# Attention to the last feed-forward of a two-layer block: first weights split early, rows normalised and two slices run per 256 rows

## Chip, cores and metric

One core of one Trainium2 chip. The metric is the device time of one execution in microseconds, median of the runs shown; less is better.

## The reference

512 rows (2 batches of 256) of width 512 go through two layers. Only the last two steps bear on the change:

```
x = x + L1_attention(layernorm(x), ctx)   # 32 query heads, 8 key and value heads of 128, 512 context rows a batch
x = x + L1_ffn(layernorm(x))              # out = (silu(x @ gate.T * s) * (x @ up.T * s)) @ down.T * s, 1376 inner columns
```

Layer 0 ahead of them is an attention with 8-bit rounding and a feed-forward with block-scaled rounding; the change leaves both alone.

## The kernel before, in words

The order of work is written out by hand, one program for each engine, joined by semaphores: TensorE (`pe`), ScalarE (`act`), VectorE (`dve`), GpSimd (`pool`), and SyncE (`sp`), which issues all transfers into one queue. Each engine takes its instructions strictly in order.

**Precision.** Layer 1 keeps about full precision by splitting each operand in two: a high part, rounded to fp32r, and a low part, raw minus high. `three` (L633 to L637) makes three matmuls of one product: high by high, high by low, low by high. Its lines L635 to L637 are those of all such products; the operand names tell them apart. The weights are split by GpSimd: a `tensor_scalar` rounds the high part, a `tensor_tensor` subtracts.

**Attention.** 32 units, one per two heads and batch (`unit(U, u, g)`), run through a software pipeline of four steps j a unit; even units are batch 0, odd ones batch 1. In one step GpSimd scales the probabilities of one 128-row tile by 1 / row sum (L1083) and may split a weight (L1072 and L1074: `wq` and `wo`). TensorE turns the tile (L668), multiplies it with the values (`pT,vt`), and projects with `wo` (`wo_sb,oT`) three units later; each pair of units waits for its `wo` split (`wo_split`). VectorE adds the projection to the rows `X` (L1393), two 128-row tiles a unit. The last iterations (units 28 to 31 and three units of drain, up to index 34) stand unrolled behind a loop.

**From attention to feed-forward.** At unit 33 VectorE takes the statistics of tiles 0 and 1 (batch 0: unit 30 was the last to add to them), at unit 34 that of tile 2, then of tile 3. `standardise(0, 4)` works out 1 / deviation of all four tiles by a chain of 11 tiny operations (L1180 to L1185) and writes the normalised rows `xhat` (L1187). `turn_rows(3, ...)` turns them tile by tile in 16 transposes (L629) into banks 4 to 7, `rows_high` (ScalarE, L926) and `rows_low` (VectorE, L1377) write the two parts into `xt_again`.

**Last feed-forward.** The inner width goes in 11 slices of 128. `gate_up1(c, p)` makes gate and up of slice c for all 512 rows: 24 matmuls of 512 columns, weights stationary, into banks p and 2 + p. ScalarE applies silu (L1005), VectorE multiplies (L1470, which waits for `u1_sums`), ScalarE rounds (L1010), VectorE subtracts (L1472), and `down1(c, p)` adds slice c into banks 4 to 7 (12 matmuls). The order on TensorE is gate_up 0, gate_up 1, down 0, then gate_up 2, down 1, and so on. GpSimd splits slice c + 1's weights: `split_gate_up` (L1126, L1128) starts slice 2 when slice 0's up sums are done (`u1_sums`), `split_down` (L1133, L1135) waits for an earlier slice's down sums. `fw` holds two slices of split weights. It lies over buffers of the attention, so its first two splits wait for the end of the attention: slice 0 for the last values product (`pv_sums`), slice 1 for the normalised rows (`ln_ready`). SyncE loads the raw weights (`ffn_raw`, six transfers of 256 KB for slices 0 and 1, L447) behind all of the attention's.

## Time and profile before

| | us |
|---|---|
| median of 3 runs | 710.75 |
| lowest, highest | 708.11, 712.8 |
| profiled execution, its own time | 712.11 |
| its span, first to last instruction | 710.0 |
| TensorE busy | 672.4 (95%) |
| VectorE busy | 525.8 (74%) |
| GpSimd busy | 457.6 (64%) |
| mean granted TensorE clock | 0.990 |

In rows of the trace, PE is the matmul side of TensorE and PEld its weight loads, DVE is VectorE, ACT ScalarE, POOL GpSimd. Times are us from the span's start. The end of a matmul is modelled, so the distance between starts tells the pace, not the duration.

### The profile page before, as it was taken

How to read it: one execution, taken by the hardware profiler on the slowest of the kernel's cores; microseconds unless marked ns; L12 is line 12 of the kernel's file. 1: busy time of each engine (PE TensorE's matmuls, PEld its weight loads, DVE VectorE, ACT ScalarE, POOL GpSimd, SP SyncE). 2: the span in 40 equal slices, each digit the busy share in tenths (PEclk: the TensorE clock that was granted, in tenths of full speed). 3: DMA queues.
4: the chain of work that ended last, by engine and by line, in shares of the span. 5: the costliest groups of instructions: out<-in, count | busy, mean ns of one | idle time of the engine just before them, and what ended most of it. 6: DMA issues, size and time to landing. Idle time of an engine off the chain costs nothing.

```text
span 710.0 us, 10983 instructions
## 1 busy us (share of the span) xinstructions
PE 672.4 (95%) x3099; PEld 494.8 (70%) x3104; DVE 525.8 (74%) x1039; ACT 362.8 (51%) x684; POOL 457.6 (64%) x401
## 2 busy tenths in 40 slices
PE   4989899899989999999999999999999999699998
PEld 2434344444566788888888888888888887588886
DVE  4977799778678888888889888888888885631113
ACT  2659444542466666665665665565665663211111
POOL 2365716424269879778878779689688554556661
PEclk9989999999999999999999999999999999999999
DMA  9885322140232113023132141221221021122221
GB/s 338 274 309 184 127 90 75 45 163 18 98 109 80 68 61 118 31 66 112 30 101 77 37 126 44 83 80 44 88 74 40 21 65 55 54 81 89 89 89 60
DMA packets 39402, 67.25 MB, mean 95 GB/s; under 512 B 3664, under 2 KB 11984, under 8 KB 38352
## 3 DMA queue, kind: packets, MB, share of 16 engines
q1 hardware_dynamic: 39376, 66.93, 28.8%
q8 instruction: 13, 0.21, 0.1%
q14 instruction: 13, 0.11, 0.0%
HBM read 57.48 MB, written 9.44 MB: 94 GB/s over the span
## 4 chain that ended last, share of the span: by engine, by line
PE 77%; DVE 10%; issue 4%; POOL 4%; ACT 3%; DMA 1%; SPq 0%; POOLq 0%; ACTq 0%; DVEq 0%
PE ps L635 16%; PE ps L637 16%; PE ps L636 16%; PE ps L703 11%; PE ps L668 7%; PE ps L503 4%; PE ps L519 4%; PE ps L566 2%; DMA X<-in_x 1%; DVE mx_amax L1244 1%; DVE mx_raw L1262 1%; DVE f L1292 1%; DVE f_amax L1287 1%; POOL wq_sb L1074 1%; PE ps L497 1%
## 5 line engine op out<-in xcount | busy, mean ns | idle before, releaser
L1083 POOL TENSOR_SCALAR prob<-prob,rinv 128x512 f32<-128x512 f32 x128 | 89.4, 699 | 79.3 <-DVE rinv L1420 79.3
L944 ACT ACTIVATE prob<-ps,nmax 128x512 f32<-128x512 f32 x128 | 88.3, 690 | 97.4 <-DVE nmax L1413 94.9
L703 PE MATMUL ps<-xt,wq_sb 128*128 128x512 f32 x384 | 103.2, 393 | 3.8 <-DVE q_cos L1428 2.1
L955 ACT CAST pT<-ps 128x512 fp32r<-128x512 f32 x128 | 75.1, 587 | 52.0 <-PE ps L668 51.0
L1413 DVE CUSTOM_DVE_ANT_0 ps<-ps,mask_sb 128x512 f32<-128x512 f32 x128 | 87.9, 686 | 6.7 <-PE ps L637 6.3
L1434 DVE TENSOR_TENSOR pT<-ps,pT 128x512 fp32r<-128x512 f32 x128 | 86.3, 674 | 2.6 <-ACT pT L955 1.7
L703 PEld LDWEIGHTS ps<-xt,wq_sb 128*128 128x128 f32 x384 | 71.6, 188 | 21.9 <-issue 4.6
L668 PE MATMUL ps<-idf,prob 128*128 128x128 f32 x512 | 76.7, 272 | 0.3 <-POOL prob L1083 0.3
L668 PEld LDWEIGHTS ps<-idf,prob 128*128 128x128 f32 x512 | 63.8, 141 | 17.0 <-POOL prob L1083 1.0
L503 PE MATMUL ps<-ctxT,wk_sb 128*128 128x512 f32 x128 | 63.4, 636 | 7.7 <-DMA ctxT<-in_ctx_cols 6.7
L1035 POOL TENSOR_TENSOR mx_raw<-mx_raw,mx_r 128x2048 f32<-128x2048 f32 (+1 forms) x9 | 30.2, 3354 | 61.4 <-DVE mx_r L1252 61.4
L519 PE MATMUL ps<-wv_sb,ctxT 128*128 128x512 f32 x128 | 58.8, 610 | 5.3 <-DVE col L1228 2.8
L635 PE MATMUL ps<-pT,vt 128*128 128x512 f32 x128 | 61.1, 477 | 0.5 <-DVE pT L1434 0.5
L1086 POOL TENSOR_TENSOR q_swp<-q_swp,ropeQ 128x512 f32<-128x512 f32 x32 | 47.1, 1472 | 17.6 <-ACT q_swp L965 17.6
L1470 DVE SCALAR_TENSOR_TENSOR int<-ps,sc,silu 128x512 f32<-128x512 f32 x11 | 8.2, 750 | 59.6 <-PE ps L637 59.6
L635 PE MATMUL ps<-wo_sb,oT 128*128 128x512 f32 x128 | 50.2, 393 | 1.7 <-DVE oT L1401 1.4
L635 PE MATMUL ps<-kt,qt 128*128 128x512 f32 x128 | 50.6, 395 | 0.9 <-DVE kt L1447 0.5
L637 PE MATMUL ps<-pT,vt 128*128 128x512 f32 x128 | 50.8, 397 | 0.0
L636 PE MATMUL ps<-pT,vt 128*128 128x512 f32 x128 | 50.3, 393 | 0.0
L637 PE MATMUL ps<-kt,qt 128*128 128x512 f32 x128 | 50.2, 392 | 0.0
L1074 POOL TENSOR_TENSOR wo_sb<-wo_raw,wo_sb 128x512 fp32r<-128x512 f32 x32 | 48.4, 1511 | 2.7
L636 PE MATMUL ps<-wo_sb,oT 128*128 128x512 f32 x128 | 50.0, 391 | 0.0
(152 smaller groups left out, 1572.2 us busy)
## 6 DMA issues: line engine op xcount, KB each, us to landing
mx_raw<-in_mxw SPq DMA_DIRECT2D x8, 1024.0 KB, 6.7
wq_raw<-in_wq SPq DMA_DIRECT2D x32, 256.0 KB, 3.1
wo_raw<-in_wo SPq DMA_DIRECT2D x32, 256.0 KB, 2.7
k_scr<-k_st SPq DMA_DIRECT2D x16, 256.0 KB, 2.0
v_scr<-v_st SPq DMA_DIRECT2D x16, 256.0 KB, 2.3
kr<-k_scr SPq DMA_DIRECT2D x16, 256.0 KB, 2.9
vr<-v_scr SPq DMA_DIRECT2D x16, 256.0 KB, 3.7
kr_swp<-k_scr SPq DMA_DIRECT2D x28, 128.0 KB, 3.3
```

Source lines behind the costliest of these rows:

```text
L503: last = mm(bank(n), wk_sb[:, i % 2, k], ctxT[:, k, b * CTX:(b + 1) * CTX], start=(k == 0), stop=(k == KD - 1))
L519: last = mm(bank(n), ctxT[:, k, i * P:(i + 1) * P], wv_sb[:, k, h * 512:(h + 1) * 512], start=(k == 0), stop=(k == KD - 1))
L635: mm(out_ap, left[0], right[0], start=first, stop=False)
L636: mm(out_ap, left[0], right[1], start=False, stop=False)
L637: return mm(out_ap, left[1], right[0], start=False, stop=final)
L668: last = nc.tensor.transpose(bank(2 + i % 2)[:, k * P:(k + 1) * P], prob[:, i, k * P:(k + 1) * P], idf[:])
L703: last = mm(query_bank(H), wq_sb[:, par, l, k], xt[:, r, k], start=(n == 0), stop=(n == 11))
L944: nc.scalar.activation(prob[:, j], bank(j % 2), ACT.Exp, bias=nmax[:, j:j + 1], scale=-1.0, accum_out=rsum[:, j:j + 1]).then_inc(exps, 1)
L955: copy(pT[:, v % 2, 0, :, i * P:(i + 1) * P], bank(2 + i % 2).rearrange("p (k c) -> p k c", k=4)).then_inc(ph_ready, 1)
L1083: nc.gpsimd.tensor_scalar(prob[:, i], prob[:, i], rinv[:, i:i + 1], 1.0, ALU.mult, ALU.mult).then_inc(probs, 1)
L1413: nc.vector.tensor_tensor_reduce(out=bank(j % 2), in0=bank(j % 2), in1=mask_sb[:, 2 * (u % 2) + j % 2], scale=-1.0, scalar=BIG, op0=ALU.ad ...
L1434: tt(pT[:, v % 2, 1, :, i * P:(i + 1) * P], bank(2 + i % 2).rearrange("p (k c) -> p k c", k=4), pT[:, v % 2, 0, :, i * P:(i + 1) * P].bitc ...
```

## The change

It does four things.

- **Buffers.** `fw` is two tensors, `fw_even` (slices 0, 2, ...) over the raw and split query weights, and `fw_odd` over the raw keys and values. These are dead before the attention ends. `silu1`, `int1` and `int1s` lie between.
- **Transfers and splits.** SyncE issues the six loads of slices 0 and 1 ahead of the last four `wo` loads. GpSimd splits them one matrix at a time (`split_early`) in units 30 (steps 1, 3), 31 (1, 3) and 32 (1, 2), each behind that step's scaling, or behind the `wo` split.
- **Rows by batch.** VectorE normalises tiles 0 and 1 right after their statistics, ahead of the last two adds, and tiles 2 and 3 after the low parts of batch 0. Transposes (`turn_batch`), high and low parts go by batch, two 128-column groups of both tiles in one bank.
- **Slices 0 and 1 by batch.** `gate_up1_batch` makes gate and up of both slices for 256 rows of batch 0 (48 matmuls of 256 columns), then for batch 1; the sums of a slice are signalled at batch 1. From slice 2 on all is as before.

```diff
@@ SyncE
+            for c in range(2):
+                for m, w in enumerate((gate_w, up_w, down_w)):
+                    sp.dma_start(ffn_raw[:, c, m], w[c]).then_inc(fw_in[c], 16)
             for U in range(NUNIT - 4, NUNIT):
                 unit(U, U % 4, NKV - 1)
...
-            sp.wait_ge(ffn0_done, NT)
-            for c in range(2):
-                for m, w in enumerate((gate_w, up_w, down_w)):
-                    sp.dma_start(ffn_raw[:, c, m], w[c]).then_inc(fw_in[c], 16)
@@ TensorE
-            pe.wait_ge(proj_added, 2 * NUNIT)
-            turn_rows(3, ROW_BANKS[1])
+            def turn_batch(b):
+
+                pe.wait_ge(ln_ready, 3 * NT + 2 * b + 2)
+                for k in range(KD):
+                    for t in range(2):
+                        lo = (k % 2) * SEQ + t * P
+                        last = nc.tensor.transpose(bank(HALF_BANK[b] + k // 2)[:, lo:lo + P],
+                                                   xhat[:, 2 * b + t, k * P:(k + 1) * P], idf[:])
+                    if k % 2 == 1:
+                        last.then_inc(xh_turned, 1)
+
+            def gate_up1_batch(c, b):
+
+                pe.wait_ge(fw_split, 2 * c + 1)
+                cols = slice(b * SEQ, (b + 1) * SEQ)
+                for m, done in ((0, g1_sums), (1, u1_sums)):
+                    for k in range(KD):
+                        if c == 0 and m == 0:
+                            pe.wait_ge(xtl_ready, KD + 2 * b + k // 2 + 1)
+                        last = three(bank(2 * m + c)[:, cols], [fw[c][:, m, s, k * P:(k + 1) * P] for s in range(2)],
+                                     [xt_again[:, s, k, cols] for s in range(2)], k == 0, k == KD - 1)
+                    if b == 1:
+                        last.then_inc(done, 1)
...
-            gate_up1(0, 0)
-            gate_up1(1, 1)
+            for b in range(BATCH):
+                turn_batch(b)
+                gate_up1_batch(0, b)
+                gate_up1_batch(1, b)
             down1(0, 0)
@@ ScalarE
-            rows_high(1, xt_again)
+            for b in range(BATCH):
+                for n in range(2):
+                    act.wait_ge(xh_turned, KD + 2 * b + n + 1)
+                    copy(xt_again[:, 0, 2 * n:2 * n + 2, b * SEQ:(b + 1) * SEQ],
+                         bank(HALF_BANK[b] + n).rearrange("p (k c) -> p k c", k=2)).then_inc(xth_ready, 1)
@@ GpSimd
+            def split_early(U, j):
+
+                c, m = divmod({(30, 1): 0, (30, 3): 1, (31, 1): 2, (31, 3): 3, (32, 1): 4, (32, 2): 5}[U, j], 3)
+                if m == 0:
+                    pool.wait_ge(fw_in[c], 48)
+                if c == 0 and m == 0:
+                    pool.wait_ge(q_sums, NH)
+                if c == 1 and m == 0:
+                    pool.wait_ge(k_split, 2 * NKV)
+                    pool.wait_ge(v_split, 2 * NKV)
+                pool.sem_inc(pool_past_wait, 1)
+                nc.gpsimd.tensor_scalar(fw[c][:, m, 0], ffn_raw[:, c, m], 1.0, 1.0, ALU.mult, ALU.mult).then_inc(fwh_ready, 1)
+                pool.wait_ge(fwh_ready, 3 * c + m + 1)
+                low = tt(fw[c][:, m, 1], ffn_raw[:, c, m], fw[c][:, m, 0].bitcast(F32), ALU.subtract)
+                if m > 0:
+                    low.then_inc(fw_split, 1)
...
-            pool.wait_ge(pv_sums, NUNIT)
-            split_gate_up(0, 0, 0)
-            split_down(0, 0)
-            pool.wait_ge(ln_ready, 4 * NT)
-            split_gate_up(1, 1, 0)
-            split_down(1, 1)
@@ VectorE
+            def rows_low_again(b):
+                cols = slice(b * SEQ, (b + 1) * SEQ)
+                for n in range(2):
+                    dve.wait_ge(xth_ready, KD + 2 * b + n + 1)
+                    tt(xt_again[:, 1, 2 * n:2 * n + 2, cols], bank(HALF_BANK[b] + n).rearrange("p (k c) -> p k c", k=2),
+                       xt_again[:, 0, 2 * n:2 * n + 2, cols].bitcast(F32), ALU.subtract).then_inc(xtl_ready, 1)
...
                             row_stats(0)
                             row_stats(1)
                             aggregate(0, 2)
+                            standardise(0, 2)
...
             row_stats(NT - 1)
             aggregate(NT - 1, NT)
-            standardise(0, NT)
-            rows_low(1, xt_again)
+            rows_low_again(0)
+            standardise(2, NT)
+            rows_low_again(1)
```

What moves, engine by engine, at the places that matter. GpSimd in the unrolled units 29 to 32 and behind them, before; L1083 scales a tile's probabilities, L1072 and L1074 split one `wo`:

```order
L1072 TENSOR_SCALAR wo_sb<-wo_raw 128x512 [waits wo_in1]
L1074 TENSOR_TENSOR wo_sb<-wo_raw,wo_sb 128x512 [waits woh_ready]
L1083 TENSOR_SCALAR prob<-prob,rinv 128x512 [waits inverse] x4
L1072 TENSOR_SCALAR wo_sb<-wo_raw 128x512 [waits wo_in0,proj_sums]
L1074 TENSOR_TENSOR wo_sb<-wo_raw,wo_sb 128x512 [waits woh_ready]
L1083 TENSOR_SCALAR prob<-prob,rinv 128x512 [waits inverse] x2
L1072 TENSOR_SCALAR wo_sb<-wo_raw 128x512 [waits wo_in1]
L1074 TENSOR_TENSOR wo_sb<-wo_raw,wo_sb 128x512 [waits woh_ready]
L1126 TENSOR_SCALAR fw<-ffn_raw 128x512 [waits pv_sums,fw_in0]
```

And now, from the same `wo` split of unit 30's pair on (L1110 scales, L1099 and L1101 split `wo`):

```order
L1099 TENSOR_SCALAR wo_sb<-wo_raw 128x512 [waits wo_in1]
L1101 TENSOR_TENSOR wo_sb<-wo_raw,wo_sb 128x512 [waits woh_ready]
L1110 TENSOR_SCALAR prob<-prob,rinv 128x512 [waits inverse]
L1150 TENSOR_SCALAR fw_even<-ffn_raw 128x512
L1152 TENSOR_TENSOR fw_even<-ffn_raw,fw_even 128x512 [waits fwh_ready]
L1110 TENSOR_SCALAR prob<-prob,rinv 128x512 [waits inverse] x2
L1150 TENSOR_SCALAR fw_even<-ffn_raw 128x512
L1152 TENSOR_TENSOR fw_even<-ffn_raw,fw_even 128x512 [waits fwh_ready]
L1110 TENSOR_SCALAR prob<-prob,rinv 128x512 [waits inverse]
L1099 TENSOR_SCALAR wo_sb<-wo_raw 128x512 [waits wo_in0,proj_sums]
L1101 TENSOR_TENSOR wo_sb<-wo_raw,wo_sb 128x512 [waits woh_ready]
```

A cast and a subtraction of `fw_even` or `fw_odd` now stand between scalings, where before the first split of `fw` came behind all of them and waited for `pv_sums`.

VectorE behind the last low part of the attention's output (`oT`), before:

```order
L1171 BN_AGGR meanvar<-stats 128x2
L1393 TENSOR_TENSOR X<-ps,X 128x512 [waits proj_sums]
L1165 BN_STATS stats<-X 128x6 [waits proj_added]
L1171 BN_AGGR meanvar<-stats 128x2 [waits ln_step]
L1393 TENSOR_TENSOR X<-ps,X 128x512 [waits proj_sums]
L1165 BN_STATS stats<-X 128x6 [waits proj_added]
L1171 BN_AGGR meanvar<-stats 128x2 [waits ln_step]
L1180 TENSOR_SCALAR var_eps<-meanvar 128x4 [waits ln_step]
```

And now, from the end of the chain of tiny operations for tiles 0 and 1:

```order
L1225 SCALAR_TENSOR_TENSOR rstd<-newton,rstd 128x2 [waits ln_step]
L1227 TENSOR_SCALAR xhat<-X,meanvar,rstd 128x512 [waits ln_step]
L1227 TENSOR_SCALAR xhat<-X,meanvar,rstd 128x512
L1439 TENSOR_TENSOR X<-ps,X 128x512 [waits proj_sums]
L1205 BN_STATS stats<-X 128x6 [waits proj_added]
L1211 BN_AGGR meanvar<-stats 128x2 [waits ln_step]
L1439 TENSOR_TENSOR X<-ps,X 128x512 [waits proj_sums]
L1205 BN_STATS stats<-X 128x6 [waits proj_added]
L1211 BN_AGGR meanvar<-stats 128x2 [waits ln_step]
L1423 TENSOR_TENSOR xt_again<-ps,xt_again 128x2x256 [waits xth_ready] x2
L1220 TENSOR_SCALAR var_eps<-meanvar 128x2 [waits ln_step]
```

The normalised rows of tiles 0 and 1 come ahead of the two adds (L1439), and the second chain begins behind the low parts of batch 0.

TensorE behind its last projection matmul, before:

```order
L637 MATMUL ps<-wo_sb,oT 128x512
L629 MATMUL ps<-idf,xhat 128x128 [waits ln_ready,proj_added]
L629 MATMUL ps<-idf,xhat 128x128 x3
L629 MATMUL ps<-idf,xhat 128x128 [waits ln_ready]
L629 MATMUL ps<-idf,xhat 128x128 x3
```

And now (L756 turns the rows of batch 0):

```order
L639 MATMUL ps<-wo_sb,oT 128x512
L756 MATMUL ps<-idf,xhat 128x128 [waits ln_ready]
L756 MATMUL ps<-idf,xhat 128x128 x7
L637 MATMUL ps<-xt_again,fw_even 128x256 [waits xtl_ready,fw_split]
L638 MATMUL ps<-xt_again,fw_even 128x256
L639 MATMUL ps<-xt_again,fw_even 128x256
```

The first feed-forward matmul now waits for half of the rows (eight transposes instead of sixteen) and has 256 columns instead of 512.

## Rows read from the trace of the kernel before

**Rows 1.** The page, chain that ended last, by engine.

```profile
PE 77%; DVE 10%; issue 4%; POOL 4%; ACT 3%; DMA 1%; SPq 0%; POOLq 0%; ACTq 0%; DVEq 0%
```

**Rows 2.** TensorE's timeline: start us, us, instruction, count, idle before.

```profile
607.04 0.39 PE L637 MATMUL ps<-wo_sb,oT 128*128 128x512 f32 x1
612.16 3.31 PE L629 MATMUL ps<-idf,xhat 128*128 128x128 f32 x16 [4.74 <-DVE xhat L1187]
616.64 0.47 PE L635 MATMUL ps<-xt_again,fw 128*128 128x512 f32 x1 [1.17 <-DVE xt_again L1377]
...
627.64 0.39 PE L635 MATMUL ps<-fw,int1s 128*128 128x512 f32 x1
```

**Rows 3.** Weight loads (PEld) at the first feed-forward matmuls, timeline.

```profile
616.61 0.19 PEld L635 LDWEIGHTS ps<-xt_again,fw 128*128 128x128 f32 x1 [1.37 <-issue]
616.72 0.19 PEld L636 LDWEIGHTS ps<-xt_again,fw 128*128 128x128 f32 x1
```

**Rows 4.** Windows: busy (count) of PE, PEld, DVE, ACT, POOL; granted clock; DMA share, GB/s.

```profile
76.00:79.00 3.00, 0.30 (x2) 0.00 (x0) 3.00 (x3) 0.66 (x1) 2.69 (x1) 1.00 0.70 229
79.00:82.00 3.00, 2.88 (x4) 1.34 (x5) 2.93 (x6) 0.00 (x0) 0.00 (x0) 0.52 0.43 180
130.00:132.00 2.00, 0.00 (x0) 0.00 (x0) 1.58 (x1) 2.00 (x3) 1.77 (x2) 1.00 0.73 262
611.00:612.00 1.00, 0.00 (x0) 0.00 (x0) 0.90 (x5) 0.00 (x0) 0.00 (x0) 0.79 0.15 55
612.00:614.00 2.00, 1.84 (x9) 1.87 (x10) 1.39 (x4) 0.00 (x0) 0.39 (x1) 0.50 0.00 0
615.00:617.00 2.00, 0.83 (x6) 0.58 (x5) 1.20 (x2) 1.81 (x4) 2.00 (x1) 1.00 0.00 0
```

**Rows 5.** Timeline of VectorE, and ScalarE's copy, after the last projection.

```profile
605.58 0.25 DVE L1171 BATCH_NORM_AGGREGATE meanvar<-stats 128x2 f32<-128x6 f32 x2
606.10 0.69 DVE L1393 TENSOR_TENSOR X<-ps,X 128x512 f32<-128x512 f32 x1 [0.27 <-PE ps L637]
...
609.29 0.17 DVE L1180 TENSOR_SCALAR var_eps<-meanvar 128x4 f32<-128x4 f32 x1
...
611.47 1.92 DVE L1187 TENSOR_SCALAR xhat<-X,meanvar,rstd 128x512 f32<-128x512 f32 x4
...
615.18 2.05 ACT L926 CAST xt_again<-ps 128x512 fp32r<-128x512 f32 x4 [12.89 <-PE ps L629]
...
615.80 2.48 DVE L1377 TENSOR_TENSOR xt_again<-ps,xt_again 128x512 fp32r<-128x512 f32 x4 [2.42 <-ACT xt_again L926]
```

**Rows 6.** GpSimd's timeline in units 30 and 31, and wo's subtraction by the page.

```profile
577.71 0.69 POOL L1083 TENSOR_SCALAR prob<-prob,rinv 128x512 f32<-128x512 f32 x1 [2.43 <-DVE rinv L1420]
578.98 0.69 POOL L1083 TENSOR_SCALAR prob<-prob,rinv 128x512 f32<-128x512 f32 x1 [0.58 <-DVE rinv L1420]
579.65 0.62 POOL L1072 TENSOR_SCALAR wo_sb<-wo_raw 128x512 fp32r<-128x512 f32 x1
...
581.67 0.69 POOL L1083 TENSOR_SCALAR prob<-prob,rinv 128x512 f32<-128x512 f32 x1
...
L1074 POOL TENSOR_TENSOR wo_sb<-wo_raw,wo_sb 128x512 fp32r<-128x512 f32 x32 | 48.4, 1511 | 2.7
```

**Rows 7.** TensorE's timeline, last turned probabilities and first projection of unit 30.

```profile
594.61 0.60 PE L668 MATMUL ps<-idf,prob 128*128 128x128 f32 x4
...
598.65 0.50 PE L635 MATMUL ps<-wo_sb,oT 128*128 128x512 f32 x1
```

**Rows 8.** Slice 0: timeline of VectorE and GpSimd, and line L1472 (min/median/max ns).

```profile
622.49 0.75 DVE L1470 SCALAR_TENSOR_TENSOR int<-ps,sc,silu 128x512 f32<-128x512 f32 x1 [4.20 <-PE ps L637]
623.92 2.88 DVE L1472 TENSOR_TENSOR int1s<-int,int1s 128x512 fp32r<-128x512 f32 x1 [0.69 <-ACT int1s L1010]
...
623.86 2.40 POOL L1128 TENSOR_TENSOR fw<-ffn_raw,fw 128x1024 fp32r<-128x1024 f32 x1
...
L1472 DVE TENSOR_TENSOR int1s<-int,int1s x11: 691/693/2876, 623.9 to 702.8; 128x512 fp32r<-128x512 f32 x11
```

More of the change, by code:

```diff
@@ L35 @@
 CH = MXT * D
-ROW_BANKS = ([4, 5, 0, 7], [4, 5, 6, 7])
+ROW_BANKS = [4, 5, 0, 7]
+HALF_BANK = (0, 4)
 STEPS = (
@@ L207, in build @@
             int1s = sb("int1s", [P, 2, 2, 512], F32R, a)
+            fw_even = sb("fw_even", [P, 3, 2, D], F32R, a)
+            fw = (fw_even, fw_odd)
             res = sb("res", [P, NT, D], F32, a)
@@ L620, in _, with turn_rows @@
             late_keys(2, range(2, 4))
-            def turn_rows(turn, banks):
+            def turn_rows():
                 for t in range(NT):
-                    if turn == 2 and t == NT - 1:
+                    if t == NT - 1:
                         late_keys(3, range(KD))
-                    pe.wait_ge(ln_ready, 4 * turn + t + 1)
+                    pe.wait_ge(ln_ready, 2 * NT + t + 1)
                     for k in range(KD):
-                        last = nc.tensor.transpose(bank(banks[k])[:, t * P:(t + 1) * P], xhat[:, t, k * P:(k + 1) * P], idf[:])
+                        last = nc.tensor.transpose(bank(ROW_BANKS[k])[:, t * P:(t + 1) * P], xhat[:, t, k * P:(k + 1) * P], idf[:])
                         if t == NT - 1:
@@ L755, in gate_up1 @@
                     for k in range(KD):
-                        if isinstance(c, int) and c == 0 and m == 0:
-                            pe.wait_ge(xtl_ready, KD + k + 1)
-                        last = three(bank(2 * m + p), [fw[:, p, m, s, k * P:(k + 1) * P] for s in range(2)],
+                        last = three(bank(2 * m + p), [fw[p][:, m, s, k * P:(k + 1) * P] for s in range(2)],
                                      [xt_again[:, s, k] for s in range(2)], k == 0, k == KD - 1)
@@ L766, in down1 @@
                     last = three(bank(4 + t), [int1s[:, p, s, t * P:(t + 1) * P] for s in range(2)],
-                                 [fw[:, p, 2, s] for s in range(2)], isinstance(c, int) and c == 0, isinstance(c, int) and c == NI - 1)
+                                 [fw[p][:, 2, s] for s in range(2)], isinstance(c, int) and c == 0, isinstance(c, int) and c == NI - 1)
                     last.then_inc(d1_sums, 1)
-            gate_up1(0, 0)
-            gate_up1(1, 1)
+            for b in range(BATCH):
+                turn_batch(b)
+                gate_up1_batch(0, b)
+                gate_up1_batch(1, b)
             down1(0, 0)
@@ L921, in _, with rows_high @@
             copy_keys(*LATE_KEYS[2])
-            def rows_high(turn, dst):
+            def rows_high():
                 for k in range(KD):
-                    act.wait_ge(xh_turned, 4 * turn + k + 1)
-                    copy(dst[:, 0, k], bank(ROW_BANKS[turn][k])).then_inc(xth_ready, 1)
+                    act.wait_ge(xh_turned, k + 1)
+                    copy(xt[:, 0, k], bank(ROW_BANKS[k])).then_inc(xth_ready, 1)
             act.wait_ge(kr_in[0], 16)
@@ L1107, in unit @@
                         split(wo_sb[:, par // 2, par % 2, 0], wo_sb[:, par // 2, par % 2, 1], wo_raw[:, par % 2], woh_ready, wo_split, H + 1)
+                    if isinstance(U, int) and (U, j) in ((30, 1), (30, 3), (31, 1), (31, 3), (32, 1), (32, 2)):
+                        split_early(U, j)
+            def split_early(U, j):
[13 more added lines that the diff above has]
+                    low.then_inc(fw_split, 1)
             pool.wait_ge(wq_in[0], 16)
```

22 lines of the change are left out of this document (11 added, 11 removed).

## The prediction

> **What bounds the kernel now.** I read the page first: the chain that ended last runs through TensorE for 77% of the span [rows 1], so a change pays only where TensorE stands still or is slow. Then TensorE's timeline from the last attention work to the last feed-forward: it starts its last projection matmul at 607.04, gets its first transpose of the normalised rows at 612.16, needs 3.31 us for 16 of them, and starts the first feed-forward matmul after another 1.17 us idle [rows 2]. The weight-load row says when a matmul really begins: the second load starts with the first matmul, at 616.72 [rows 3]. The first down projection starts at 627.64 [rows 2]: 48 matmuls of 512 columns in 10.92 us, 0.2275 each. After that TensorE has no gap to the end, so the change is worth exactly what it moves this 627.64. Third, the granted clock [rows 4]: it fell near 611.6, stood at 0.50 (1.2 GHz) from 612 to 614, and was full from 615 on. Fourth, VectorE, which fills the 4.7 us hole: adds and statistics, a chain of tiny operations from 609.29 to 611.47, then four normalisations in 1.92 us [rows 5].
>
> **The change, part by part.**
>
> Early splits on GpSimd. Six splits of 128x512 move from behind the attention into units 30 to 32, and each delays the row scalings behind it. A scaling takes 0.67 (578.98 to 579.65), a split 2.02 (579.65 to 581.67) [rows 6]. From 577.71, GpSimd now has eight scalings (units 30 and 31) and six splits (E0 to E3 of the change, two of wo): 8 x 0.67 + 6 x 2.02 = 17.5, so the last scaling ends at 595.2. TensorE transposed it at 594.61 [rows 7]: 0.6 late, 0.7 with the signal. Two more splits (E4, the last of wo) end at 599.2, and the projection of unit 30, which now waits for that wo, started at 598.65 [rows 7]: again 0.7. Both are the same delay, not two, because the second wait only fills what the first has shifted. The other scalings have more room than they lose. Bounds: 0, since waiting can't gain, and 2.2, if in each of the eight splits the subtraction takes the kernel's mean of 1.511 [rows 6], some 0.2 more than 2.02 leaves for it. I take **+0.7**, from the nearest rows. The transfers of these weights move ahead of four wo loads that are issued two units before their use, so they cost nothing; without that cover they would cost their few us once. Removing the late splits gains nothing: the first feed-forward matmul waited for rows, not for weights [rows 2].
>
> Normalising two tiles first. Statistics of tiles 0 and 1 end at 605.83 [rows 5]. The chain (2.2 us, read from 609.29 to 611.47) and two normalisations (2 x 0.48) now follow at once, up to 609.0. Behind them wait, on VectorE, the two adds with statistics that ran from 606.10 to 609.26, 3.2 us of work [rows 5]: to 612.2. Only then come the low parts of batch 0, and the first matmul begins 0.92 after the first of these starts (615.80 to 616.72) [rows 3, 5]: 613.1. Transposes and copies of batch 0 end before 612 and are hidden. With +0.7: **613.8, where it was 616.72, a gain of 2.9**.
>
> Slices 0 and 1 by batch. 48 matmuls of 512 columns become 96 of 256. A pair can't be faster than its weight load: 0.11, from the load at 616.61 to the matmul at 616.72 [rows 3]. The 512-column step of 0.2275 is 0.213 of columns at 2.4 GHz plus 0.014, so 256 columns give 0.107 + 0.014 = 0.12. No row shows this shape; the bounds are 0.11 (load alone) and 0.22 (load and columns in turn). I take 0.12, as loads are fully hidden at 512. So batch 0 takes 5.8.
>
> Clock. TensorE will stand still for 1.8 us, work 0.9, then stand still for 3.1. An idle of 2 us (130 to 132) left the clock full, and it was down from 79 on after 2.7 idle us in the three before [rows 4]. I assume that it falls and stays down for 3 us, as here, partly over the hole: **1.2** lost (bounds 0 and 3 us at half speed, 1.5). Batch 0 then ends at 613.8 + 5.8 + 1.2 = 620.8.
>
> Transposes of batch 1. They stand behind batch 0 in TensorE's order. Four transposes at 0.11 and 0.25 to drain give 0.7, then the copy, the low part and the start take 615.18 to 616.72, 1.5 [rows 3, 5]: **2.2** in which no matmul of the sum runs, from 620.8 to 623.0. Before, they cost nothing here. VectorE's second chain and normalisations (3.2 us after 614.7) are hidden by batch 0; if batch 0 were under 4 us, they would be late next. Batch 1 takes 5.8: **628.8, 1.2 later than 627.64**.
>
> The first slice's inner product. The down projection of slice 0 waits for its split. Now the sums of slice 0 end in the middle of batch 1, at 623.0 + 2.9, and VectorE starts on them 0.3 later, at 626.2. Before, this was 622.49, and the split ended at 626.80, 4.31 later, because VectorE's subtraction took 2.88 instead of 0.69: GpSimd's 2.40 us subtraction had started 0.06 earlier [rows 8]. Of eleven, it is the only slow one [rows 8]. Before, 24 matmuls (5.5 us) covered the 4.31. Now only 24 half ones (2.9) do, and the same signal starts both engines. So the down projection starts at 626.2 + 4.31 + 0.1 = **630.6, 3.0 later than 627.64**. Steps further on are those of before, among which TensorE had no gap, and their distances don't change.
>
> The Trainium skill, page "SBUF — State Buffer", section "Who interferes with whom", calls the port pair that VectorE and GpSimd share an exclusive lock, taken by whoever issues first, and names a VectorE operation with two SBUF inputs as one that needs it. The 2.88 agrees with it. By that rule a subtraction that starts 0.06 earlier would not wait, and the end would be 1.2 later rather than 3.0.
>
> The page "TensorE: Matmul & The Clock Gate", section "Back-to-back issue gap", gives 131 ns as the sustained step at 512 columns and 81 at 128. By it a 256-column step would be under 0.10, by my estimate 2 us less for 96. This trace has 227 ns at 512, so the page's steps don't hold for these four-byte operands, and the sum doesn't use them.
>
> **Sum.** The profiled execution took 712.11 with a span of 710.0, 2.1 around it; with +3.0 it would be 715.1. It lies 1.4 above the median 710.75, from which I count: 710.75 + 3.0 = **713.7**. A measurement of this kernel can tell about 1%, 7.1 us, from no change; the runs before spread from 708.11 to 712.8. This is no measurable change.
>
> **Rivals.**
> - VectorE gets the port first (0.2). The margin is 0.06 us, against it that both engines start from one signal and keep their order. Then only the row work decides: +1.2, 711.9.
> - The clock stays up (0.2), since work lies in the hole now. For it: the idle of 2 us; against: the 2.7, which 3.1 exceeds [rows 4]. Then -1.2: 712.5, and with the port won as well 710.7.
> - Weight loads exposed: slower (0.08). Mechanism: at 256 columns the load (0.11) is as long as the matmul, and any part that doesn't overlap shows on 96 pairs. At 0.213 per pair: 613.8 + 1.2 + 2.2 + 20.4 = 637.6, which is +10.0, 720.7. It decides above 1% from 0.183 per pair on. For it: no slack; against: at 512 the exposed part is 0.014.
> - The splits crowd GpSimd more than I count (0.07): +2.2 instead of +0.7, 715.2.
>
> **How the numbers follow.** The forecast has 0.45. The range takes the best case less a little (710.7 with the spread of a median, 709.8) and the crowded case plus as much and some exposure (716.6). Faster by over 1% needs 7.1 us, and the idle time of TensorE in this place is 4.74 + 1.17 [rows 2], under 6: 0.02. Slower by over 1% needs exposed loads, and most of them: 0.06. The rest, 0.92, is within 1%.
>
> **What would show it.** In the profile of the changed kernel: the 256-column matmuls 0.12 apart; the first about 3 us sooner after the last projection than before (607.04 to 616.72 is 9.7; now 6.1); an idle or transposing stretch of 2.2 between the batches; a slow VectorE subtraction at slice 0 and TensorE idle some 1.7 us before the first down projection; a clock dip that now lies over matmuls; the last probabilities 0.6 later on GpSimd. The forecast is wrong if that idle is missing while the span still grows, if the steps are above 0.13, or if the attention shifts by over 1.5.

## The result and the profile after

Over 17 runs each, the changed kernel takes 714.97 us (713.23 to 716.92) and the kernel before 711.88 us (707.9 to 714.25): ratio 1.0044, 95% interval 1.0029 to 1.0060, or +3.1 us (+2.1 to +4.3). The forecast was 713.7, +3.0, within 1%. Direction and size are right. One of its terms, the loss to TensorE's clock, is too small, and the profile shows it once two executions are put on one clock.

The chain that ended last, page of the changed kernel:

```profile
PE 75%; DVE 11%; issue 5%; POOL 5%; ACT 3%; DMA 1%; SPq 0%; POOLq 0%; DVEq 0%; ACTq 0%
```

Of the chain, TensorE lost 2% and VectorE, GpSimd and issue gained 1% each [rows 1]: TensorE waits more than before. Where, its timeline tells (start us, us, instruction, count, idle before):

```profile
607.18 0.39 PE L639 MATMUL ps<-wo_sb,oT 128*128 128x512 f32 x1
609.24 1.09 PE L756 MATMUL ps<-idf,xhat 128*128 128x128 f32 x8 [1.67 <-DVE xhat L1227]
612.97 0.55 PE L637 MATMUL ps<-xt_again,fw_even 128*128 128x256 f32 x1 [2.64 <-DVE xt_again L1423]
...
620.80 1.03 PE L756 MATMUL ps<-idf,xhat 128*128 128x128 f32 x8
622.89 0.36 PE L637 MATMUL ps<-xt_again,fw_even 128*128 128x256 f32 x1 [1.05 <-DVE xt_again L1423]
...
630.55 0.47 PE L637 MATMUL ps<-fw_even,int1s 128*128 128x512 f32 x1 [1.67 <-DVE int1s L1519]
...
709.35 0.39 PE L639 MATMUL ps<-fw_even,int1s 128*128 128x512 f32 x1
```

These answer [rows 2]. The first feed-forward matmul comes 5.8 us after the last projection (before 9.6). From there to the first down projection it is 17.6 us (before 11.0). Of the idle times in brackets, 1.67 at 609.24 is the wait for the normalised rows, 2.64 is the wait for the low parts of batch 0 (ScalarE's copies were done at 611.00, but VectorE was at its adds and statistics until 612.2), 1.05 is the round trip of batch 1's turned rows over ScalarE and VectorE, and 1.67 at 630.55 is the wait for the inner product.

**A common clock.** The distance from the span's start to a given attention step differs between executions, before anything that the change touches. I count from the first scaling of unit 30, called the mark: 577.71 in before [rows 6], 577.01 here.

```profile
577.01 0.69 POOL L1110 TENSOR_SCALAR prob<-prob,rinv 128x512 f32<-128x512 f32 x1 [2.43 <-DVE rinv L1467]
...
593.89 0.69 POOL L1110 TENSOR_SCALAR prob<-prob,rinv 128x512 f32<-128x512 f32 x1
...
597.22 1.30 POOL L1101 TENSOR_TENSOR wo_sb<-wo_raw,wo_sb 128x512 fp32r<-128x512 f32 x1
```

From the mark, the last projection stands at 30.17 (before 29.33), the first feed-forward matmul at 35.96 (38.93), the first down projection at 53.54 (49.93), and the last matmul of all at 132.34 (128.61). So from the mark to the last matmul the change costs 3.7 us. The spans differ by only 3.0 (713.0 against 710.0), because the mark itself came 0.7 us sooner in this execution. The medians (+2.1 to +4.3) hold both values.

VectorE's and GpSimd's timelines at the rows and at slice 0, which answer [rows 5, 8], and line L1519 by itself (min/median/max ns):

```profile
612.17 1.26 DVE L1423 TENSOR_TENSOR xt_again<-ps,xt_again 128x512 fp32r<-128x512 f32 x2
...
615.50 1.00 DVE L1227 TENSOR_SCALAR xhat<-X,meanvar,rstd 128x512 f32<-128x512 f32 x2
...
627.57 2.83 DVE L1519 TENSOR_TENSOR int1s<-int,int1s 128x512 fp32r<-128x512 f32 x1 [0.69 <-ACT int1s L1033]
...
627.49 2.37 POOL L1174 TENSOR_TENSOR fw_even<-ffn_raw,fw_even 128x1024 fp32r<-128x1024 f32 x1
...
L1519 DVE TENSOR_TENSOR int1s<-int,int1s x11: 691/693/2831, 627.6 to 705.8; 128x512 fp32r<-128x512 f32 x11
```

GpSimd again starts its subtraction 0.08 us before VectorE's, and VectorE's takes four times its median, now with TensorE waiting for it. The granted clock, in windows (busy and count of PE, PEld, DVE, ACT, POOL; clock; DMA share, GB/s), answers [rows 4]:

```profile
609.00:611.00 2.00, 1.09 (x8) 0.85 (x8) 1.93 (x5) 1.07 (x2) 0.00 (x0) 0.92 0.00 0
611.00:613.00 2.00, 0.03 (x1) 0.06 (x1) 1.93 (x5) 0.01 (x1) 0.00 (x0) 0.50 0.00 0
613.00:615.00 2.00, 2.00 (x9) 2.00 (x10) 1.72 (x10) 0.00 (x0) 0.00 (x0) 0.50 0.00 0
615.00:617.00 2.00, 2.00 (x12) 2.00 (x11) 1.40 (x5) 0.00 (x0) 0.00 (x0) 0.50 0.00 0
617.00:619.00 2.00, 2.00 (x16) 2.00 (x16) 0.00 (x0) 0.00 (x0) 0.00 (x0) 0.87 0.00 0
```

At 0.50 the matmuls of 256 columns stand 0.213 us apart, at 1.00 they stand 0.12 apart. Added up over quarter-microsecond windows, 6.8 us lie at half clock; before it was 3.4.

### The profile page after: what moved, and what is told of

The parts are those of the page before. It is cut to its first block, busy times and chain, and to the rows that moved or that the text cites. A ratio compares the mean times of both kernels' runs of the same rounds, so it can differ in the third digit from the quotient of the medians.

```text
span 713.0 us, 11100 instructions
## 1 busy us (share of the span) xinstructions
PE 673.4 (94%) x3152; PEld 497.1 (70%) x3152; DVE 527.5 (74%) x1050; ACT 362.9 (51%) x684; POOL 458.0 (64%) x403
## 4 chain that ended last, share of the span: by engine, by line
PE 75%; DVE 11%; issue 5%; POOL 5%; ACT 3%; DMA 1%; SPq 0%; POOLq 0%; DVEq 0%; ACTq 0%
PE ps L637 16%; PE ps L639 15%; PE ps L638 15%; PE ps L705 11%; PE ps L670 7%; PE ps L505 4%; PE ps L521 4%; PE ps L568 2%; DMA X<-in_x 1%; DVE mx_amax L1284 1%; DVE mx_raw L1302 1%; POOL prob L1110 1%; DVE stats L1205 1%; DVE f L1332 1%; DVE f_amax L1327 1%
## 5 line engine op out<-in xcount | busy, mean ns | idle before, releaser
L1110 POOL TENSOR_SCALAR prob<-prob,rinv 128x512 f32<-128x512 f32 x128 | 89.4, 699 | 73.7 <-DVE rinv L1467 73.6
L670 PEld LDWEIGHTS ps<-idf,prob 128*128 128x128 f32 x512 | 63.8, 141 | 17.5 <-POOL prob L1110 1.6
L1101 POOL TENSOR_TENSOR wo_sb<-wo_raw,wo_sb 128x512 fp32r<-128x512 f32 x32 | 48.4, 1513 | 2.7
```

The source lines that it names most:

```text
L670: last = nc.tensor.transpose(bank(2 + i % 2)[:, k * P:(k + 1) * P], prob[:, i, k * P:(k + 1) * P], idf[:])
L1110: nc.gpsimd.tensor_scalar(prob[:, i], prob[:, i], rinv[:, i:i + 1], 1.0, ALU.mult, ALU.mult).then_inc(probs, 1)
```

## Experiments

Each was timed beside the kernel before; the ratios rest on 6 to 12 executions of each of its relatives (17 of the changed kernel), the distances on one profiled execution. All distances are us from the mark of the same execution. "Low" is the time at half clock between 603 and 624 us.

| kernel | ratio to before, 95% | last projection | first ff. matmul | last matmul | low |
|---|---|---|---|---|---|
| before | | 29.33 | 38.93 | 128.61 | 3.4 |
| changed | 1.0044 (1.0029 to 1.0060) | 30.17 | 35.96 | 132.34 | 6.8 |
| e1_no_meeting | 1.0025 (1.0004 to 1.0045) | 30.18 | 35.97 | 131.59 | 6.8 |
| e2_kept_busy | 0.9999 (0.9979 to 1.0019) | 30.18 | 35.97 | 130.29 | 0 |
| e3_splits_behind | 1.0057 (1.0035 to 1.0078) | 29.33 | 36.02 | 132.38 | 6.8 |
| e4_turn_inside | 1.0031 (1.0010 to 1.0052) | 30.09 | 35.88 | 131.08 | 6.8 |
| e5_splits_alone | 1.0048 (1.0029 to 1.0068) | 30.17 | 39.80 | 131.63 | 10.2 |
| e6_before_busy | 0.9989 (0.9972 to 1.0006) | 29.35 | 37.60 | 127.26 | 0 |
| e8_sub_later | 1.0061 (1.0041 to 1.0080) | 30.15 | 35.93 | 130.47 | 6.8 |
| e9_splits_in_gaps | 1.0067 (1.0044 to 1.0089) | 29.83 | 35.61 | 132.16 | 6.8 |
| e10_combined | 0.9952 (0.9931 to 0.9973) | 29.81 | 35.59 | 126.72 | 0 |
| e11_low_parts_first | 0.9973 (0.9950 to 0.9996) | 29.86 | 34.12 | 126.17 | 0 |
| e12_one_more | 1.0077 (1.0049 to 1.0104) | 30.25 | 36.04 | 132.85 | 6.8 |
| e13_before_again | one run, 709.05 us | 29.35 | 38.71 | 128.36 | 3.4 |

(In e9 the marked scaling is itself 0.19 late behind a split; the distances allow for it.) The ratios carry 0.2% either way, 1.4 us, so single terms are read from the distances and the ratios only check the sum.

**e1_no_meeting.**

```diff
+                    if j == 0:
+                        pool.wait_ge(int1_split, 1)
                     split_gate_up(2 * it + j, j, it)
```

> The changed kernel, but GpSimd begins the split of slice 2 only when VectorE has finished splitting the inner product of slice 0. Theory (the two engines' subtractions meet: VectorE's 128x512 subtraction took 2.83 us beside GpSimd's 2.37, elsewhere 0.69): it takes 0.7 us again, the first down projection starts 1.8 us earlier (some 1.9 us after GpSimd's is gone nothing else is late, since slice 2's weights are wanted only some 6 us later), and the time is the changed kernel's 715.0 less 1.8, near 713.2. Rival 1 (the subtraction is slow for another reason, such as its operands): it stays at 2.8 us and the time at 715.0. Rival 2 (GpSimd's splits of the early slices become the bound once they start 2 us later): the subtraction falls to 0.7 us, but a gap of up to 2 us opens before the gate matmuls of slice 2 and the time stays at 715.

VectorE's subtractions of slices 0 and 1, GpSimd's, and TensorE at the start of slice 2:

```profile
627.54 0.69 DVE L1521 TENSOR_TENSOR int1s<-int,int1s 128x512 fp32r<-128x512 f32 x1 [0.69 <-ACT int1s L1033]
...
630.40 2.40 DVE L1521 TENSOR_TENSOR int1s<-int,int1s 128x512 fp32r<-128x512 f32 x1 [0.69 <-ACT int1s L1033]
...
629.87 2.38 POOL L1174 TENSOR_TENSOR fw_even<-ffn_raw,fw_even 128x1024 fp32r<-128x1024 f32 x1
...
632.39 0.49 PE L637 MATMUL ps<-xt_again,fw_even 128*128 128x512 f32 x1 [0.79 <-POOL fw_even L1174]
```

The theory on the cause holds: with GpSimd elsewhere the same instruction takes 0.69, and the down projection starts at 51.8 instead of 53.5. The second rival holds in part: TensorE gives 1.0 of these 1.8 back at slice 2, where it waits for GpSimd (0.79). The meeting has also moved, to slice 1's subtraction (2.40). The last matmul is 0.75 sooner.

**e8_sub_later** keeps GpSimd's two copies where they were and lets only its subtraction wait.

```diff
                 pool.wait_ge(fwh_ready, 3 * c + 2)
+                pool.wait_ge(int1_split, 1)
                 tt(fw[p][:, 0:2, 1], ...
```

> The changed kernel with a milder form of the wait of e1_no_meeting: GpSimd makes the two rounded copies of slice 2's weights at once, and only its subtraction waits until VectorE has split the inner product of slice 0. In e1_no_meeting the subtraction of VectorE took 0.69 us and the first down projection started 1.8 us earlier (51.8 us after the mark against 53.5), but the gate matmuls of slice 2 then stood 0.8 us for GpSimd, VectorE's next subtraction met GpSimd's (2.40 us), and the last matmul came only 0.75 us earlier (131.59 against 132.34). Theory (that was the price of 1.2 us of copies that need not wait): GpSimd's subtraction runs from about 628.3 to 630.7 on the changed kernel's clock, no gap before slice 2, last matmul at 132.34 less 1.8, near 130.6, time 715.0 less 1.8, near 713.2. Rival (VectorE's subtraction of slice 1 takes the meeting over and the loss appears before the down projection of slice 1): last matmul between 131.3 and 132.3.

The last matmul moves by 1.87, as expected: this is the whole price of the meeting. The time didn't follow (ratio 1.0061, where 713.2 us had been expected and 715.77 came). In this profile and in that of e1_no_meeting, 5.7 us pass from the start of the last matmul to the end of the span, in all others 3.6 to 3.7. The transfers of e1_no_meeting, 709 to 711 us, and those of the changed kernel in the same window (queue: packets, MB, share; then the issues: count, KB, us to landing):

```profile
q8 instruction: 1, 0.02, 5.2%
out<-res SPq DMA_DIRECT2D x2, 256.0 KB, 3.3
```

```profile
q1 hardware_dynamic: 336, 0.62, 83.9%
out<-res SPq DMA_DIRECT2D x3, 256.0 KB, 2.1
```

In these two executions a block of instructions is fetched while the output is stored, and the end comes 2 us later; that the fetch is the cause is not shown. Nor need it be so in every execution: the profiled one of e1_no_meeting took 716.22 us, and its median is 713.63.

**e12_one_more** asks whether one more instruction at GpSimd's end does that.

```diff
             split_down(NI - 1, 0)
+            pool.wait_ge(fw_split, 2 * NI)
```

> The changed kernel with one more instruction at the end of GpSimd's program: a wait for a count that its own last subtraction has reached. In e1_no_meeting and e8_sub_later the last matmul came 0.75 and 1.87 us earlier than in the changed kernel, but the span was 1.2 and 1.1 us longer: from the start of the last matmul to the end it took 5.7 us, in every other kernel 3.6 to 3.7, and the profile has one transfer of instructions (0.02 MB) at 709 to 711, beside the last two output transfers. Theory (one instruction more on GpSimd pushes its program over the edge of a block that is fetched when the program ends, and this costs 2 us at the end): last matmul unchanged at about 132.3 after the mark, 5.7 us from it to the end, time 2.0 above the changed kernel, 717. Rival (the late fetch comes from the wait in the middle of the program, or from chance): 3.7 us from the last matmul to the end, time 715.

This does not decide it. The profiled execution has no late fetch, 3.67 us from the last matmul to the end, which speaks for the rival. But it took 713.23 us and was the shortest of six; their median, 717.19, is what the theory gave, though the ratio's interval overlaps the changed kernel's. What decides the late fetch, and how often it comes, stays open. e2_kept_busy, e4_turn_inside, e10_combined and e11_low_parts_first also fetched one block more than the changed kernel, but before the last matmul, and their ends take the usual 3.7 us.

**e2_kept_busy.**

```diff
+            def keep_warm(n):
+                for _ in range(n):
+                    mm(bank(3), oT[:, 1, 0, 0:P], wo_sb[:, 1, 1, 0], start=True, stop=True)
+            keep_warm(7)
             for b in range(BATCH):
                 turn_batch(b)
+                if b == 0:
+                    keep_warm(11)
                 gate_up1_batch(0, b)
```

> The changed kernel with 7 extra 128x512 matmuls (results thrown away, in a bank that is free) between the last projection and the transposes of the first batch, and 11 more between these transposes and the first 256-column matmul. Theory (TensorE's granted clock falls to half at 610.7 because the engine stands idle for most of 607.5 to 613, and 21 matmuls of the first batch then run 0.21 us apart instead of 0.12): the granted clock stays at 1.00, the spacing is 0.12 from the first, and the time is 715.0 less 2.0, near 713.0. Rival 1 (the slow first matmuls wait for something else, such as their weight loads, and the clock row only goes along with it): spacing stays near 0.21, time 715. Rival 2 (the extra matmuls end late and push the first batch back): the clock stays up but the gain is given back in part, between 713.5 and 715.

```profile
604.43 1.75 PE L752 MATMUL ps<-wo_sb,oT 128*128 128x512 f32 x7
606.27 1.09 PE L760 MATMUL ps<-idf,xhat 128*128 128x128 f32 x8
607.11 2.78 PE L752 MATMUL ps<-wo_sb,oT 128*128 128x512 f32 x11
610.00 0.35 PE L637 MATMUL ps<-xt_again,fw_even 128*128 128x256 f32 x1
610.19 0.28 PE L638 MATMUL ps<-xt_again,fw_even 128*128 128x256 f32 x1
610.31 0.28 PE L639 MATMUL ps<-xt_again,fw_even 128*128 128x256 f32 x1
```

The granted clock reads 1.00 in every window and the step is 0.12 from the first. The first real matmul is where it was (35.97), so the extra work displaces nothing, and the last matmul comes 2.05 sooner. The prediction had this term at 1.2 and bounded it by 1.5. The Trainium skill, page "TensorE: Matmul & The Clock Gate", section "Part 1: The HAM clock gate", has the clock halved while the engine idles and given back under load; this run agrees (18 extra matmuls, 0 against 6.8 us of low clock).

**e6_before_busy** puts 20 such matmuls ahead of before's sixteen transposes.

> The kernel before, with 20 extra 128x512 matmuls (results thrown away) between the last projection and the sixteen transposes. Before's granted clock was down to 0.50 over 612 to 614 us, over the transposes alone. Theory (keeping TensorE busy keeps its clock, and in before only transposes ran slow): the transposes start to give their banks sooner, the first matmul comes about 1.0 us earlier, and the time is 711.9 less 1.0, near 710.9, so that about 1.0 of the changed kernel's loss to the clock (2.0 us) is new and the rest was there before in another place. Rival (the transposes' way is set by VectorE and ScalarE behind them, one tile at a time, and not by their own speed): first matmul within 0.3 us, time 711.9. Rival 2 (20 matmuls end after 612.2 and push the transposes back): up to 0.4 us later.

First matmul 1.33 sooner, last matmul 1.35 sooner. So before lost 1.3 us to the clock, ahead of its first matmul, and the changed kernel 2.0, behind it. In the changed kernel the first matmul stands at 35.96 with the clock low and at 35.97 with it full. So of the 3.0 us by which the change brings this matmul forward, 1.3 are before's loss to the clock, and only 0.7 of the 2.0 is more than before lost.

**e13_before_again** is the kernel before, unchanged.

> The kernel before, unchanged, for a second profile. Its first profile had a granted clock of 0.50 from 611.4 to 614.9 us (3.5 us, over the transposes alone); the changed kernel and the five of its relatives without extra matmuls had one of 6.8 us, and e5_splits_alone, whose rows go as in before, one of about 10 us that reached over ten 512-column matmuls. Theory (how long the clock stays down after TensorE has stood idle varies from one execution to the next, and before's 3.5 us was a short one): a dip of another length, with slow 512-column matmuls behind the transposes. Rival (it is fixed by what the kernel does): again 3.5 us and no slow 512-column matmul.

```profile
609.38 3.38 PE L629 MATMUL ps<-idf,xhat 128*128 128x128 f32 x16 [4.74 <-DVE xhat L1187]
613.61 0.47 PE L635 MATMUL ps<-xt_again,fw 128*128 128x512 f32 x1 [0.85 <-DVE xt_again L1377]
```

This agrees with the rival: 3.4 us low again, over transposes only. The distances of before repeat to 0.25 us. e12_one_more has the changed kernel's order and differs only in GpSimd's last instruction, and there the last matmul comes 0.51 later: its clock fell 34.8 us from the mark instead of 33.7 and was low over 26 matmuls instead of 21. So where the clock falls, a difference under 0.5 us between two profiles can't be told from chance, and the changed kernel's loss to the clock was 2.0 in one execution and about 2.5 in another (five more steps of 0.213 instead of 0.12).

**e3_splits_behind.**

```diff
-                    if isinstance(U, int) and (U, j) in ((30, 1), (30, 3), (31, 1), (31, 3), (32, 1), (32, 2)):
-                        split_early(U, j)
...
+            for n in range(6):
+                split_early(n // 3, n % 3)
```

> The changed kernel with the six early splits moved behind all of GpSimd's attention work (they then run from about 598 to 610.5 us). Rows, slices and buffers stay as changed. Theory (the early splits delay attention: the changed kernel's scalings were 0.71 us earlier than before's at 561 to 577 us, and its last projection 0.14 later, so 0.85 was lost in between): the last projection comes 0.85 us earlier against the same run's 577 us mark, and the time is 715.0 less 0.85, near 714.1. Rival 1 (the 0.7 us lead at 577 us comes and goes between executions, and the splits cost only the 0.14 seen at the end): time 714.9. Rival 2 (the splits now stand beside the normalisation on VectorE and slow it, or slice 1's are not ready at 617): the statistics or the first matmuls come up to 1 us later and the time is 715 or above.

```profile
605.19 1.29 POOL L1149 TENSOR_TENSOR fw_odd<-ffn_raw,fw_odd 128x512 fp32r<-128x512 f32 x1
...
605.43 1.07 DVE L1220 TENSOR_SCALAR var_eps<-meanvar 128x2 f32<-128x2 f32 x1
...
606.60 0.39 PE L639 MATMUL ps<-wo_sb,oT 128*128 128x512 f32 x1
609.56 1.09 PE L756 MATMUL ps<-idf,xhat 128*128 128x128 f32 x8 [2.57 <-DVE xhat L1227]
```

Attention returns to 29.33, so the early splits cost it 0.84. Yet nothing is gained: an operation on two numbers a row, 0.17 us in the changed kernel, took 1.07 beside GpSimd's last subtraction, and the first transposes stand at 32.29 (changed 32.23). This is the second rival. GpSimd had started 0.24 us before VectorE, and both ended together (606.48 and 606.50). The Trainium skill, page "SBUF — State Buffer", section "Who interferes with whom", counts `tensor_scalar` among the operations that can take the port pair shared with GpSimd, when their operands allow it, and says that issue order and not shape decides who blocks; the 1.07 agrees.

**e9_splits_in_gaps** moves two splits into the idle 2.4 us ahead of units 30 and 31, and four behind unit 31.

```diff
-... in ((30, 1), (30, 3), (31, 1), (31, 3), (32, 1), (32, 2)):
+... in ((30, 0), (31, 0), (32, 0), (32, 1), (32, 2), (32, 3)):
```

> The changed kernel with its six early splits in other places of GpSimd's attention work: two in the gaps of 2.4 us that follow the fourth scaling of units 29 and 30, four behind the last scaling of all, so that they end at about 603 us, before the first batch is normalised (about 605.7). In e3_splits_behind, where all six stood behind, the last projection came back to 29.33 us after the mark, but the first step of the normalisation met a split (1.07 us instead of 0.17) and the transposes came at 32.29 as in the changed kernel (32.23). Theory (a place exists where the splits cost nothing): last projection at 29.33, first step of the normalisation 0.17, transposes at 31.4, last matmul at 132.34 less 0.84, near 131.5, time 715.0 less 0.8, near 714.2. Rival (a split in a gap of 2.4 us still delays the scaling behind it, or the splits at 597 to 603 meet VectorE's subtractions of the last unit): last projection at 29.6 or later and less than 0.5 us gained.

The rival holds: attention still loses 0.5. The last split of `wo` now stands behind two others, and the projection that waits for it comes late (e10_combined shows the rows). The first matmul gains 0.35; the last gains 0.18, which is less than one profile can tell.

**e5_splits_alone** has early transfers, splits and buffers as changed, rows and slices as before.

> The early splits, the early transfers and the new buffers as in the changed kernel, but rows and the first two slices as before (one normalisation of all four tiles, sixteen transposes, 512 columns). Counted from the start of the first scaling of unit 30 on GpSimd (577.71 us in before, 577.01 in the changed kernel) the last projection matmul stood at 29.33 us in before, 30.17 in the changed kernel and 29.33 with the splits behind attention. Theory (the early splits cost attention 0.84 us and nothing else of them is on the path): last projection at 30.17, last matmul of all at 128.61 + 0.84 = 129.45 against that mark (before: 128.61), time 711.9 + 0.8 = 712.7. Rival (with one normalisation the end of attention has slack that takes the delay in, or GpSimd's idle end of attention lets VectorE's subtraction of the inner product run clear of a second subtraction and gives the 0.8 us back): last matmul within 0.3 of 128.6, time 711.9.

```profile
600.00:625.00 25.00, 18.30 (x70) 0.80 0.03 12
...
614.36 0.63 PE L638 MATMUL ps<-xt_again,fw_even 128*128 128x512 f32 x1
614.78 0.63 PE L636 MATMUL ps<-xt_again,fw_even 128*128 128x512 f32 x1
```

Attention loses 0.84, as expected, and the first matmul 0.87. The last matmul loses 3.0, because here the clock stays low for 10.2 us and eleven matmuls of 512 columns start in it, most of them 0.43 apart instead of 0.23. Neither theory had that. Whether it comes from this kernel or from the execution, one profile can't say; its ratio (1.0048) is that of a kernel which usually loses it.

**e4_turn_inside.**

```diff
-            for b in range(BATCH):
-                turn_batch(b)
-                gate_up1_batch(0, b)
-                gate_up1_batch(1, b)
+            turn_batch(0)
+            gate_up1_batch(0, 0)
+            turn_batch(1)
+            gate_up1_batch(1, 0)
+            gate_up1_batch(0, 1)
+            gate_up1_batch(1, 1)
```

> The changed kernel with TensorE's order changed: transposes of the second batch's rows stand between the two slices of the first batch, so that the copies and subtractions that follow them run beside the second of these slices. No wait is changed. Theory (of the 2.1 us between the two batches 1.03 are the transposes and the other 1.06 a round trip over ScalarE and VectorE that stands bare): the round trip goes, the transposes stay, and the time is 715.0 less 1.1, near 713.9. Rival (the rows of the second batch are normalised only at 616.5, and the engine comes to their transposes at about 617 with a clock that is still low, so that these take about twice as long, or the longer low clock returns part of it): time between 714.2 and 715.0.

```profile
618.84 1.03 PE L756 MATMUL ps<-idf,xhat 128*128 128x128 f32 x8
619.62 0.36 PE L637 MATMUL ps<-xt_again,fw_odd 128*128 128x256 f32 x1
```

No idle time is left between the batches, only the 1.03 us of the transposes, and the last matmul comes 1.26 sooner.

**e10_combined** joins the four: GpSimd's splits (one behind unit 30, the others behind unit 31, slice 1's gate and up with one subtraction), the waiting subtraction, the extra matmuls, and this order:

```diff
+            keep_warm(7)
+            turn_batch(0)
+            keep_warm(11)
+            gate_up1_batch(0, 0)
+            gate_up1_batch(1, 0, [0])
+            turn_batch(1)
+            gate_up1_batch(1, 0, [1])
+            gate_up1_batch(0, 1)
+            gate_up1_batch(1, 1)
```

> The changed kernel with what the earlier runs taught: early splits where they meet nothing (one in the gap behind the last scaling of unit 30, the rest behind unit 31, the gate and up weights of slice 1 with one joint subtraction, so that GpSimd's program is no longer than in the changed kernel); the wait of e8_sub_later; 7 and 11 extra matmuls that keep TensorE's clock; and the second batch's transposes inside the first batch's matmuls of slice 1, between gate and up. Against the first scaling of unit 30: last projection 29.33 (changed 30.17), first 256-column matmul 35.1 (35.96), then 96 steps of 0.12 and 1.03 of transposes, first down projection 47.8 (53.54; before 49.93), last matmul near 126.5 (132.34; before 128.61). Theory (the four costs are separate and add up: 0.84 + 2.0 + 1.06 + 1.8): time 2.1 below before, 3.5 to 5.8 below the changed kernel, ratio to before 0.997. Rival 1 (with the others gone the rows of the second batch, normalised only about 3.5 us after the first matmul, hold the transposes, or another meeting of VectorE and GpSimd appears): last matmul between 127.5 and 128.6, ratio 0.999 to 1.000. Rival 2 (a longer program costs 2 us at the end, as in e8_sub_later, where a fetch of instructions lay between the last output transfers): ratio 1.000.

```profile
613.29 0.35 PE L637 MATMUL ps<-xt_again,fw_even 128*128 128x256 f32 x1
617.67 1.04 PE L760 MATMUL ps<-idf,xhat 128*128 128x128 f32 x8
618.47 0.36 PE L637 MATMUL ps<-xt_again,fw_odd 128*128 128x256 f32 x1
...
625.74 0.40 PE L637 MATMUL ps<-fw_even,int1s 128*128 128x512 f32 x1
```

707.88 us against 712.05 of before, timed beside it: with e11_low_parts_first the only version here whose interval lies below before's time, by 0.5% and 0.3%. From the first feed-forward matmul to the first down projection it is 12.45 us without a gap, where the changed kernel took 17.6 and before 11.0. The last projection is still 0.48 late, for the reason seen in e9_splits_in_gaps: the last split of `wo` ends at 599.07 and the matmul starts behind it. (The view names VectorE's `oT` as what ended the wait, but that was done at 598.58.)

```profile
597.79 1.28 POOL L1111 TENSOR_TENSOR wo_sb<-wo_raw,wo_sb 128x512 fp32r<-128x512 f32 x1
...
599.17 0.47 PE L637 MATMUL ps<-wo_sb,oT 128*128 128x512 f32 x1 [0.56 <-DVE oT L1461]
```

**e11_low_parts_first.**

```diff
                             aggregate(2, 3)
+                            rows_low_again(0)
```

> As e10_combined, and VectorE makes the low parts of the first batch's rows before it adds the last projection and takes its statistics, not after (5 extra matmuls instead of 11 behind the first transposes). Theory (the first 256-column matmul waits for these two subtractions, which stood behind 1.5 us of work on the second batch): it starts 1.4 us earlier, 33.7 us after the mark; the second batch's rows are ready no earlier than before, so TensorE stands some 0.65 us before their transposes, and the last matmul comes 0.8 us before that of e10_combined, near 125.7; ratio to before 0.996. Rival (the second batch's rows come later by what the first's gained, or the copies of ScalarE are not ready when VectorE asks): last matmul as in e10_combined or later.

```profile
614.72 1.09 PE L760 MATMUL ps<-idf,xhat 128*128 128x128 f32 x8 [0.72 <-DVE xhat L1241]
```

The first matmul comes 1.47 sooner than in e10_combined, 0.72 of it is given back here, and the last matmul gains 0.55 (0.8 expected). The medians don't show it: 709.62 against 707.88, with overlapping intervals.

## Why the prediction was right, point by point

- **Attention +0.7**: 0.84, by the distances and by e3_splits_behind. From the mark to the end of the last scaling the working gave 17.5, and 577.01 to 594.58 is 17.6. One reading was off: the projection of unit 30 (598.76) did not wait for its `wo` split, which ended at 598.52, but for VectorE's `oT`, which ended at 598.70 and which the late probabilities had delayed. It is one delay, as I counted it, by another way. The rival with crowded splits falls: the subtractions took 1.30, not 1.51.
- **First matmul**: forecast at 36.1 from the mark (613.8 less 577.71). Its second weight load starts at 613.11, which is 36.1:

```profile
613.11 0.33 PEld L638 LDWEIGHTS ps<-xt_again,fw_even 128*128 128x128 f32 x1
```

- **Step of 0.12**: measured 0.12 at full clock, 0.21 only where the clock was at half, so the rival with exposed weight loads falls.
- **Clock, 1.2 (bounds 0 and 1.5)**: this is the step that failed. I assumed that the clock "falls and stays down for 3 us, as here". It stayed down for 6.8, of which 4.5 lay over matmuls: 21 steps of 0.213 instead of 0.12 are 2.0, and e2_kept_busy gives 2.05. So the value and its upper bound of 1.5 were both too low. The assumption carried a duration from one pattern of work to another. The rival that the clock stays up falls too. Why it stays low for longer here than in before is not shown.
- **Transposes of batch 1, 2.2**: 2.1 (620.80 to 622.89). e4_turn_inside shows that the round trip (1.05) was avoidable; the transposes (1.03) stay.
- **The first slice's inner product**: forecast 4.4 from VectorE's start on the sums to the down projection; from that start (626.13) to 630.55 is 4.4. e1_no_meeting and e8_sub_later show that the meeting of the two subtractions is the cause and that it costs 1.8 to 1.9. The order of the two did not turn, so the rival with VectorE first falls.
- **Sum**: from the mark, the down projection was forecast at 630.6 less 577.71, 52.9, and came at 53.54. The difference of 0.65 is, within 0.1, the 0.8 that the clock took beyond its term less the 0.1 that the transposes give back. The last matmul lost another 0.12.

That the medians differ by 3.1, so close to the forecast 3.0, is in part luck: in the profiles the changed stretch costs 3.7, and the interval (2.1 to 4.3) can't tell the two apart.

The change set out with the right hole, and gained 3.8 us there (9.6 to 5.8). It gave back 0.84 in attention and 6.6 behind the hole: 2.0 to the clock, 2.1 to the transposes of batch 1 and a round trip that had no cover, 1.9 to the meeting and its wait (what is left over; e1_no_meeting and e8_sub_later give 1.8), and 0.6 to the pace of 256 columns (11.5 for 96 against 10.9 for 48).

## What to carry to other kernels

Work moved forward into a hole takes its waits along: each stage of half the size has half the cover for the same fixed round trip, so put the next stage's transposes between the matmuls of this one. Where TensorE must idle before a dense stretch, try throw-away matmuls in a free bank: here they cost nothing and kept its clock. Before a split or copy is moved, look at which operations of the other engine it will stand beside there, tiny ones too.

## What the runs showed of the hardware that I had not expected

- One idle stretch was followed by very different times at half clock: 3.4 us (before, twice), 6.8 (the changed kernel and six relatives), 10.2 (e5_splits_alone, whose rows go as before's), and 0 in all four kernels with extra matmuls.
- VectorE's tiny operation on 2 columns took 1.07 us beside GpSimd's subtraction (e3_splits_behind), and 0.17 without it.
- Executions differ by more than 4 us before the change begins: the mark lay between 573.57 and 578.12 (e9_splits_in_gaps, less its 0.19). It goes for the most part with the time at half clock in the first 100 us: 573.57 with none, 574.03 and 575.34 with 3.4 us, 574.61 to 577.27 with 6.8, 577.70 to 578.12 with 10.2. That one causes the other is not shown. Windows of before (mark 577.71), then of e5_splits_alone (mark 573.57): busy of PE, clock, DMA share, GB/s:

```profile
0.00:50.00 50.00, 37.62 (x92) 0.93 0.89 313
50.00:100.00 50.00, 46.94 (x170) 0.97 0.44 146
```

```profile
0.00:50.00 50.00, 37.31 (x109) 1.00 0.88 312
50.00:100.00 50.00, 46.75 (x166) 1.00 0.46 153
```

- A fetch of instructions beside the last stores went with 2.05 us more between the last matmul and the end, in two of fourteen profiles; what places it there, and whether it is the cause, is open.
